# The first group of a pass: key parts and query ahead of the next rows' statistics

## What is computed

```python
qkv = x @ w_qkv.T
q, k, v = split(qkv)                      # 16 heads of 32
q = relu(q); k = relu(k)
ksum = k.sum(over rows)
z = 1.0 / (einsum('bhd,bhdn->bhn', ksum, q) + eps)
context = einsum('bhdn,bhen->bhde', v, k)
out = einsum('bhde,bhen->bhdn', context, q) * z
return out @ w_proj.T + b_proj
```

## Time and profile before

| | |
|---|---|
| median of three executions | 2459.85 us (2457.72 to 2460.81) |
| the profiled execution | 2460.71 us, its span 2458.9 us |
| TensorE busy | 2400.0 us, 98% of the span |
| VectorE, ScalarE, GpSimd busy | 1805.9, 1580.2, 1136.8 us |
| mean granted TensorE clock | 0.992 of full |

### The profile page before, as it was taken

The page is one execution under the profiler, slowest core; times in us unless marked ns, Lnnn a source line. Parts: engine busy times, 40 slices in busy tenths (PEclk is TensorE's granted clock), DMA queues, the critical chain, the costliest instruction groups (busy, mean ns, idle before and its releaser), DMA issues.

```text
span 2458.9 us, 56923 instructions
## 1 busy us (share of the span) xinstructions
PE 2400.0 (98%) x20208; PEld 1433.9 (58%) x20208; DVE 1805.9 (73%) x3548; ACT 1580.2 (64%) x3473; POOL 1136.8 (46%) x929
## 2 busy tenths in 40 slices
PE   5999999998999999999999999999999999999997
PEld 2444444454666666666666666666666666666664
DVE  5444444426888888888888888888888888888885
ACT  3222323226777777777777777777777777777774
POOL 2587533313444444444444444444444444444444
PEclk9999999999999999999999999999999999999999
DMA  5634434311111111111111111111111111111111
GB/s 137 202 99 126 103 103 102 85 56 35 40 47 47 51 43 47 43 43 43 43 44 50 50 45 48 43 43 43 43 43 47 50 48 46 43 43 43 43 29 32
DMA packets 250704, 145.65 MB, mean 59 GB/s; under 512 B 208096, under 2 KB 208096, under 8 KB 250144
## 3 DMA queue, kind: packets, MB, share of 16 engines
q1 hardware_dynamic: 240048, 119.32, 19.6%
q10 hardware_dynamic: 9504, 17.31, 1.9%
q0 software_dynamic: 1104, 8.40, 0.9%
HBM read 61.09 MB, written 33.55 MB: 38 GB/s over the span
## 4 chain that ended last, share of the span: by engine, by line
PE 93%; POOL 3%; DVE 2%; ACT 1%; issue 1%; DMA 1%; POOLq 0%; SPq 0%; DVEq 0%; ACTq 0%
PE psum L319 17%; PE psum L320 16%; PE psum L321 16%; PE psum L592 6%; PE psum L457 5%; PE psum L494 5%; PE psum L447 4%; PE psum L474 4%; PE psum L503 3%; PE psum L514 2%; PE psum L331 2%; PE psum L368 2%; PE psum L367 2%; PE psum L466 2%; PE psum L366 1%; PE psum L429 1%
## 5 line engine op out<-in xcount | busy, mean ns | idle before, releaser
L319 PE MATMUL psum<-wb,region 128*128 128x512 f16 x768 | 293.0, 381 | 0.0
L320 PE MATMUL psum<-wb,region 128*128 128x512 f16 x768 | 291.6, 380 | 0.0
L321 PE MATMUL psum<-wb,region 128*128 128x512 f16 x768 | 291.6, 380 | 0.0
L1077 POOL TENSOR_TENSOR region<-region,kfac 128x512 f32<-128x512 f32 x64 | 66.7, 1042 | 482.9 <-DVE kfac L1335 482.9
L1060 POOL TENSOR_TENSOR region<-region 128x1024 f32<-128x1024 f32 x64 | 147.8, 2309 | 258.7 <-DVE region L1443 230.2
L1443 DVE SCALAR_TENSOR_TENSOR region<-psum,region 128x512 f16<-128x512 f32 x64 | 44.2, 691 | 222.4 <-ACT region L887 222.4
L1065 POOL TENSOR_TENSOR region<-region 128x1024 f32<-128x1024 f32 x64 | 150.5, 2352 | 93.2 <-DVE region L1208 93.2
L1072 POOL TENSOR_SCALAR region<-region,m 128x512 f32<-128x512 f32 x256 | 172.3, 692 | 26.5 <-DVE hm L1279 26.5
L592 PE MATMUL psum<-region 128*128 128x512 f16 x768 | 176.2, 379 | 2.1 <-DVE region L1443 2.1
L1081 POOL TENSOR_TENSOR region<-region 128x512 f32<-128x512 f32 x64 | 81.8, 1277 | 202.7 <-ACT region L795 202.7
L1242 DVE SCALAR_TENSOR_TENSOR region<-psum,m,region 128x512 f32<-128x512 f32 x192 | 144.1, 751 | 6.8
(11 more groups left out here) (236 smaller groups left out, 7208.3 us busy)
## 6 DMA issues: line engine op xcount, KB each, us to landing
region<-x_in SPq DMA_DIRECT2D x128, 256.0 KB, 2.6
q_cols<-region ACTq DMA_DIRECT2D x64, 256.0 KB, 2.5
region<-q_cols SPq DMA_DIRECT2D x64, 256.0 KB, 2.8
out_rows<-region SPq DMA_DIRECT2D x62, 256.0 KB, 2.0
region<-wb_in POOLq DMA_DIRECT2D x1, 3072.0 KB, 13.4
region<-wqkv_in SPq DMA_DIRECT2D x4, 512.0 KB, 6.9
region<-region SPq DMA_TRANSPOSE x128, 3.0
region<-ws_in POOLq DMA_DIRECT2D x1, 1280.0 KB, 7.6
```

Source lines behind the costliest of these rows:

```text
L319: mm(out, lhs(0), rhs(0), start=start, stop=False)
L320: mm(out, lhs(0), rhs(1), start=False, stop=False)
L321: return mm(out, lhs(1), rhs(0), start=False, stop=stop)
```

## The change

The first two groups of the first pass are written out ahead of the loop on ScalarE and VectorE, with the loop starting at group 2. In the first of them, group 0, the order on both engines differs; group 1 keeps its order. On ScalarE `key_high(now)` and `query(g, t)` come ahead of `norm_tile(now + 5)`; on VectorE `key_low(now)` comes ahead of `tile_stats`. TensorE's, GpSimd's and SyncE's instructions are the same.

```diff
@@ ScalarE
-            def group(g, p, ahead=True, more=True):
+            def group(g, p, ahead=True, more=True, first=False):
                 for t in range(GT):
                     next_p, next_t = (1 - p, t + 1) if t < GT - 1 else (p, 0)
                     go = more if t == GT - 1 else ahead
                     now = g * GT + t
-                    if go:
+                    if go and not first:
                         norm_tile(now + GT + 1)
                     key_high(now)
+                    if go and first:
+                        query(g, t)
+                        norm_tile(now + GT + 1)
                     if go:
                         high(now + GT + 1, next_p * GT + next_t, now)
-                    query(g, t)
+                    if not first:
+                        query(g, t)
                 store_q(g)
...
-            with act.Fori(0, GROUPS, 2) as g:
+            group(0, 0, first=True)
+            group(1, 1)
+            with act.Fori(2, GROUPS, 2) as g:
                 group(g, 0)
                 group(g + 1, 1)
@@ VectorE
+                    if first:
+                        key_low(now)
                     if go:
                         tile_stats(next_g, next_t)
-                    key_low(now)
+                    if not first:
+                        key_low(now)
                     if go:
                         tile_normed(next_g, next_p, next_t)
...
-            with dve.Fori(0, GROUPS, 2) as g:
+            group(0, 0, first=True)
+            group(1, 1)
+            with dve.Fori(2, GROUPS, 2) as g:
```

## The result

The changed kernel takes 2464.95 us (median of 20 executions, 2462.82 to 2468.74), the kernel before 2459.12 us (20 executions, 2455.24 to 2461.03). The ratio is 1.0024, 95% interval 1.0017 to 1.0031: 5.8 us slower. The profiled execution of the changed kernel took 2462.86 us, the second lowest of its 20, and that of the kernel before 2460.71 us, 1.6 above its median.

What follows compares the result with a forecast made beforehand. TensorE, busy for 98% of the span, bounds the kernel. Profiled 2460.71 + 0 + 0 + 5.1 (idle) + 1.4 (lower clock) = 2467.2 us, less 0.86 for the median: 2466.4; range 2459.0 to 2469.3.

Steps and rivals of the forecast that it cites:

- the likeliest case: TensorE stalls long before tile 5's queries, waiting for late stores: 2463.1 to 2469.3 us, chance 0.72.
- Key parts earlier: Group 0: tile 0's key parts come some 2 us earlier, but TensorE's moments still stand behind its queries: gain 0.
- Statistics later and loop written out: Group 0's later norm_tile is hidden, over 2 us of cover per tile; written-out rows run on half-idle engines: 0.
- The stores issued later: End of group 0: four stores behind norm_tile(8) and high(8), issued from 60.7 us instead of 58.89, 1.78 later.
- the bracket: Stores' issue from about 59.9 us if ScalarE's sequencer passes high without waiting for its end; 60.7 was taken.
- One packet of each queue in turn: DMA engines alternate queues by packet whatever the size, so 2 KB store rows go one per 24.6 KB load row.
- The rival in which stores pass as blocks: Each store waits for one large row at most, through by 67.8 us: 2459.9, no change; 0.19 including early stores.
- The landing: Group 0's stores, 286 packets left at 64 us, land behind the 3 MB load at 75.0, bounds 73.2 to 76.5.
- The stall: TensorE idles before tile 5's queries, waiting for tile 4's query: 5.1 us, 3.3 to 6.6 by the bounds.
- The clock: Lower granted clock on TensorE's 12 queries behind the idle time: 1.4 us lost, bounds 0 and 2.8.
- The sum: Profiled execution 2460.71 + 0 + 0 + 5.1 + 1.4 = 2467.2 us; for the median 2466.4.
- The threshold: Delay starts to cost at a landing of 69.9 us: 6 packets per engine left, some 96, half a microsecond.

Runs made afterwards that it cites:

- changed kernel with spaced loads: Changed kernel, GpSimd's first weight loads waiting for group 0's landed stores, the second loads behind add_keys(8) instead of add_keys(5): 2459.82 us, ratio 1.0003.
- only the stores late: Kernel before, in group 0's last tile alone query ahead of norm_tile(8) and high(8), so the stores follow these: 2463.82 us, ratio 1.0022.
- only the stores put back: Changed kernel, group 0's four stores directly behind the last query, ahead of norm_tile(8) and high(8): 2460.69 us, ratio 1.0006.
- the load in short rows: Changed kernel, the 3 MB load written as 12 rows of 2 KB per partition: 2463.65 us, ratio 1.0020.
- the control: Kernel before, only a wait added on GpSimd: first weight loads issued once group 0's four stores have landed: 2466.31 us, ratio 1.0029.
- the key parts alone: Changed kernel, query back behind high in group 0, norm_tile still behind key_high: 2466.84 us, ratio 1.0033.
- the early moments: Kernel before, tile 0's key parts further up, TensorE's tile 0 moments ahead of its queries: 2459.94 us; first loads behind stores, second behind add_keys(8): 2457.21.
- the load 7.8 us later: Changed kernel, GpSimd's first weight loads, the 3 MB among them, behind add_keys(4) instead of add_keys(3): 2474.44 us, ratio 1.0068.
- the three gated kernels: First weight loads wait for group 0's landed stores: in the changed kernel 2466.79 us, with TensorE's tile 0 moments ahead of queries 2461.88, in the kernel before 2466.31.

## Why the prediction was right

The forecast was 2466.4 us with slower as the likeliest, and the likeliest case came, at 2464.95.

- *Key parts earlier, worth 0.* Right. The high part of tile 0 runs 3.3 us earlier (28.92 against 32.19), more than the 2 us of the forecast, and TensorE took nothing from it. Only with TensorE's own order changed was 2.4 us of use to be had.
- *Statistics later and loop written out, worth 0.* Right as far as shown, by the changed kernel with spaced loads: ratio 1.0003 (0.9994 to 1.0012), and no new wait in its rows.
- *The stores issued later.* Right in kind. The trace decides the bracket: ScalarE issued them at 60.25, 0.05 us after `high` began, not at 60.7 after its end. The kernel with only the stores late had the whole loss (2463.82), and the one with only the stores put back has no stall, and no loss clear of its interval (2460.69).
- *One packet of each queue in turn.* Right: 16 against 16 in 66 to 67, and in 65 to 73 us 125 packets of q10 against 114 of q0. (From 64 to 65, as the large rows came in, it was 68 against 18.) The rival in which stores pass as blocks fell. By the Trainium skill ("DMA: Bandwidth & Descriptors", Queues, rings and completion order) an engine drains some 9 to 17 descriptors of one queue in a turn. An estimate from that figure, with a packet of the trace as one descriptor: the 36 packets that the stores have on each engine would pass in three or four turns. The trace doesn't agree: beside the load's 8 large rows on an engine 12 packets passed, and the rest behind them. The size of a turn could not be varied, since the load in short rows came out as long rows again.
- *The landing.* The stores were issued from 60.25 to 62.45 and landed 13.0 us later in the median; the `query` started at 75.55, so the last had landed by then. The forecast was 75.0, and that it came so near is in part luck, since its count was wrong. It had 286 packets left at 64. The first packet moved only at 62.2, 2 us after the issue, though the stores were issued 0.45 sooner than forecast; 194 of the 576 were through at 64, and 382 were left. Of these 193 moved from 64 to 73, 12 on an engine where I had 8, and 189 behind the load's rows, again 12 on an engine where I had up to 10. In return the large rows were through by 73.5, and not at 73.9 + 0.7: 73.9 is the load's landing, which comes later than its last row.
- *The stall.* 4.72 us measured, 5.1 forecast. The queries restarted at 76.20 where I had 75.9, but the stretch ahead was itself 0.49 us late: tile 1's moments begin at 42.83 and tile 4's at 66.14, where it was 42.34 and 65.65 before. That arises in tile 0, by the clock: its queries began 0.93 us sooner (29.67 against 30.60), but took 5.07 us at a granted clock of 0.50 instead of 3.97 at 0.64, and its moments 0.32 more. It isn't the change's doing: the tile 0 queries of the control, which has the order of before, took 4.99 us (35.13 - 30.14), and those of the key parts alone, with the changed order, 4.33 (34.56 - 30.23).
- *The clock.* 1.70 us on 12 queries, 1.4 forecast. The granted clock was 0.53 against the 0.54 of the earlier trace rows.
- *The sum.* Stall and clock make 6.4 us, 6.5 forecast; the medians differ by 5.8. Of the 1.45 us by which 2466.4 is too high, 0.73 comes from the start: the median of three executions was 2459.85, that of 20 is 2459.12. The profiled spans differ by only 1.8, by the clock in the three stretches named above; why it was higher there is open.
- *The threshold was too generous.* I had the delay begin to cost at half a microsecond of delay, counted over all 16 engines. The stores issued 0.2 us closer to the load than before already gave a stall of 1.8 us, since one engine that is behind holds all four stores. The kernel before stands nearer to this edge than I said, and the early moments fell over it from TensorE's side.

Several expectations behind the prediction were wrong, two of them in a telling way: the key parts alone (I left out that the last `query` then waits behind `high(8)`), and the load 7.8 us later (I looked at one meeting of transfers and made another). The same second meeting broke the expectations for the three gated kernels, the control among them. What I took for its cause ahead of the last two kernels, one small row for each large row for 25 us, is not what the queues show. The early moments, without the gate and with spaced loads, both came out slower than I expected.

## What to carry to other kernels

When instructions of an engine are reordered, look at the DMA issues that stand last in its loop: here a delay of 1.4 us cost 6.4 in the trace and 5.8 in the medians, since it brought a small store against a large load, while no cost was found of the operations that were moved on purpose. A transfer of 2 KB rows beside one of 24 KB rows advanced one row per large row here, and its slowest engine set its landing. Give it a lead, and count the lead per engine. Moving the large load instead is no free cure: it must stay clear of the transfers on its other side too, and a control with the gate alone shows what the gate costs.

## What the runs showed of the hardware

- One load of 256 KB on SyncE took 13.70 and 16.93 us to issue, instead of 0.34, in stretches in which all queues moved little (0.49 and 1.06 MB in 80 to 90 us, instead of 2.68): an issue can itself wait.
- In the control's stretch the DMA engines were busy without moving much: 0.31 us for a packet of q1 instead of 0.03. Such a stretch came in the profiled executions of the four kernels whose second set of loads was issued 6.5 to 10 us behind the 3 MB load, and not at 14 us or more. The cause is open.
- ScalarE began its DMA issues 0.05 us after the start of the activation ahead of them, which took 0.63.
- The clock stayed full behind 1.8 us of idle time and was at about 0.53 behind 4.7 us; behind 3.5 us the 12 queries took as long (4.29 us) as behind 4.7.
- A load described as rows of 2 KB that lie together went out in rows of 24.6 KB.
- With these two sets of large loads 8 to 10 us apart, the 12 executions of one kernel spread over 19 to 23 us, instead of 7.5 in 29 of the kernel before.
